# Two-layer graph block on one core: the scores' cross parts go through the attention's trip in DRAM

## The reference, cut to what matters

```
u     = h @ h.T / sqrt(384)
a     = softmax(u);  delta = a * adj
attn  = delta / (sum(delta) + 1e-10)
hl, hs, hr = h @ Wl.T + bl, h @ Ws.T + bs, h @ Wr.T + br
ctx   = (attn * upper) @ hl + diag(attn) * hs + (attn * lower) @ hr
h     = relu(layernorm(ctx, 1e-12) * g + beta)      # twice
out   = layernorm(x + h, 1e-5)
```

## Time and profile before

| | |
|---|---|
| median of 3 runs | 1637.04 us (1635.62 to 1637.73) |
| profiled execution, its own time | 1637.5 us |
| its span, first to last instruction | 1635.7 us |
| TensorE, VectorE, GpSimd, ScalarE busy | 98%, 91%, 73%, 58% of the span |
| granted TensorE clock, mean | 0.996 |
| DMA, mean busy share of 16 engines | 43% |
| one steady iteration, read from the timeline | 12.44 us |

### The profile page before, as it was taken

One profiled execution on the slowest core, in us unless ns is written; L12 is line 12 of the kernel. 1 busy time (PEld: TensorE's weight loads), 2 busy tenths in 40 slices (PEclk: granted clock), 3 DMA queues, 4 the chain that ended last, 5 costly groups with the idle time before them and its releaser, 6 DMA issues.

```text
span 1635.7 us, 35455 instructions
## 1 busy us (share of the span) xinstructions
PE 1609.5 (98%) x9505; PEld 1601.3 (98%) x9505; DVE 1491.4 (91%) x4628; ACT 951.4 (58%) x2451; POOL 1202.1 (73%) x1541
## 2 busy tenths in 40 slices
PE   8999999999999999999999999999999999999995
PEld 7999999999999999999999999999999999999995
DVE  7799999999999999999999999999999999999987
ACT  5565665556566556556656655665665556566553
POOL 5677777777777777777777777777777777777763
PEclk9999999999999999999999999999999999999998
DMA  4344444444444444444444444444444444444431
GB/s 158 94 116 107 111 111 112 106 113 114 107 114 109 111 107 113 114 107 114 110 110 107 112 115 107 114 111 110 108 111 115 107 114 111 110 109 110 114 83 44
DMA packets 463515, 178.61 MB, mean 109 GB/s; under 512 B 348545, under 2 KB 462593, under 8 KB 463490
## 3 DMA queue, kind: packets, MB, share of 16 engines
q1 hardware_dynamic: 463490, 178.32, 43.1%
HBM read 112.34 MB, written 65.86 MB: 109 GB/s over the span
## 4 chain that ended last, share of the span: by engine, by line
PE 91%; DVE 2%; DMA 1%; POOL 1%; SPq 1%; ACT 1%; issue 1%; DVEq 0%; POOLq 0%; ACTq 0%
PE p_proj L427 70%; PE p_gather L514 15%; PE p_score L421 5%; PE p_score L443 1%; DMA rows_mem<-rows_blocks 1%; DMA attnT_whole<-attn_mem 1%; SPq L366 1%; SPq L351 1%; POOL rstd L1164 0%; POOL proj_split L283 0%; POOL attnT L1154 0%; POOL attnT_split L1160 0%; DVE stats L626 0%; ACT normed L961 0%; DVE stats L672 0%
## 5 line engine op out<-in xcount | busy, mean ns | idle before, releaser
L427 PE MATMUL p_proj<-w,hT_layer 128*128 128x384 f32 x6912 | 1371.6, 339 | 0.2 <-DVE proj L697 0.2
L427 PEld LDWEIGHTS p_proj<-w,hT_layer 128*128 128x128 f32 x6912 | 1165.9, 189 | 0.5 <-DVE proj L697 0.5
L283 POOL TENSOR_TENSOR proj_split<-proj,proj_split 128x768 fp32r<-128x768 f32 x253 | 467.6, 1848 | 276.9 <-ACT proj_split L957 276.9
L957 ACT ACTIVATE proj_split<-proj 128x768 fp32r<-128x768 f32 x256 | 214.9, 839 | 394.9 <-DVE proj L697 393.8
L514 PE MATMUL p_gather<-proj_split,attnT_split 128*128 128x384 f32 x1536 | 309.2, 335 | 3.0 <-POOL attnT_split L1160 2.4
L514 PEld LDWEIGHTS p_gather<-proj_split,attnT_split 128*128 128x128 f32 x1536 | 270.0, 188 | 4.9 <-POOL attnT_split L1160 4.1
L1164 POOL TENSOR_TENSOR rstd<-veps,neg_half 128x1 f32<-128x1 f32 x384 | 211.2, 550 | 75.3 <-DVE veps L635 61.8
L697 DVE TENSOR_TENSOR proj<-p_proj,bias_all 128x768 f32<-128x768 f32 x256 | 245.1, 957 | 12.0 <-PE p_proj L427 4.4
L421 PE MATMUL p_score<-hT_layer 128*128 128x256 f32 x768 | 216.8, 283 | 2.0 <-DVE rows L729 2.0
L1154 POOL TENSOR_TENSOR attnT<-attnT_whole,sides 128x256 f32<-128x256 f32 x249 | 184.5, 741 | 41.0 <-DMA attnT_whole<-attn_mem 39.0
L1160 POOL TENSOR_TENSOR attnT_split<-attnT,attnT_split 128x256 fp32r<-128x256 f32 x256 | 190.3, 743 | 5.8 <-ACT attnT_split L948 5.8
(11 more groups left out here) (67 smaller groups left out, 1568.2 us busy)
## 6 DMA issues: line engine op xcount, KB each, us to landing
xt_raw<-xT SPq DMA_DIRECT2D x128, 192.0 KB, 2.5
xn<-x SPq DMA_DIRECT2D x128, 192.0 KB, 2.4
out<-o SPq DMA_DIRECT2D x128, 192.0 KB, 2.0
rows_mem<-rows_blocks SPq DMA_DIRECT2D x124, 192.0 KB, 1.9
rowsT<-rows_mem SPq DMA_DIRECT2D x496, 48.0 KB, 2.4
adj_layer<-adj SPq DMA_DIRECT2D x256, 64.0 KB, 1.9
attn_mem<-attn_blocks SPq DMA_DIRECT2D x124, 128.0 KB, 1.7
attnT_whole<-attn_mem SPq DMA_DIRECT2D x496, 32.0 KB, 2.2
```

The lines of the kernel that those rows point to most:

```text
L283: op.tensor_tensor(proj_split[u][:, LO], proj[u][:, UP:LOW + 1, :], proj_split[u][:, HI].bitcast(F32), ALU.subtract).then_inc(s_proj_lo[k], 1)
L427: return nc.tensor.matmul(p_proj[:, which, 0:D], hT_of(k, b)[:, slot, st, c, :], w[:, k, which, mv, c, :], start=(n == 0), stop=(n == 8))
L957: nc.scalar.activation(proj_split[u][:, HI], proj[u][:, UP:LOW + 1, :], ACT.Copy).then_inc(s_proj_hi[k], 1)
```

## The change

What it does, part by part:
- The two layers' score products stand in one PSUM bank (`parts`), and in steady state all six are issued within layer 1's self projection (`pair_slice`): layer 1 of graph i + 2 (before: i + 1, one iteration later) and layer 2 of graph i - 2. Layer 1's inputs get four slots in place of two, and are prepared an iteration earlier.
- ScalarE copies both cross parts at once (`copy_cross`, 256 columns); VectorE transposes them in blocks (`turn_cross`); they go with the attention's blocks through DRAM (256 KB stored, four loads of 64 KB). In the next iteration GpSimd adds the transposed cross parts to the plain ones (`add_cross`), and `scaled_scores` of both layers read that sum. The cross matmul is left in `fill` and `close` only.
- The orders on VectorE, ScalarE and GpSimd are changed: scores of both layers and the output's mean stand ahead of the sides' bias, both masks and diagonals behind `block_rows`; on ScalarE the exponentials stand ahead of `normalise_rows`.
- The output's mean comes from the accumulator of the sum x + h, and its variance from a pass of squares on ScalarE, in place of VectorE's statistics.
- The first layer's bias is loaded by DMA to all partitions, in place of a TensorE product with ones; the lists of `close` are reordered; a score product waits for the previous `scaled_scores` instead of the previous `diagonal`.

```diff
+        crossed = sb("crossed", [P, 2, N])
+        cross_sum = sb("cross_sum", [P, 2, N])
+        blocks = sb("blocks", [P, 2, 4, N])
+        whole = sb("whole", [P, 4, N])
...
+        parts = [p_score[0][:, 0:2, :], p_score[0][:, 2:4, :]]
+        cross_parts = p_score[0].rearrange("p (k t) n -> p k t n", t=2)[:, :, LO, :]
+        E = [p_score[1][:, 0, :], p_score[1][:, 1, :]]
...
# SyncE
+            def store_swap(i, slot):
+                first, last = swapped(i)
...
+                elif last == 4:
+                    sp.wait_ge(s_cross_blocks, i - 3)
...
+                sp.dma_start(swap_mem[slot][:, first:last], blocks[:, slot, first:last]).then_inc(
+                    s_swap_out[slot], 16)
+            def load_swap(i, slot):
+                first, last = swapped(i)
+                sp.wait_ge(s_swap_out[slot], swap_moves(i, slot))
+                pieces = swap_mem[slot].rearrange("(r a) k (s b) -> s a k r b", a=B, b=B)
...
+                        sp.dma_start(whole[rows_s, first:last, :].rearrange("a k (r b) -> a k r b", b=B),
+                                     pieces[s][:, first:last]).then_inc(s_swap_in[slot], 16)
# TensorE
+            def pair_slice(b0, slot0, b1, slot1, n):
+                if n == 2:
+                    done(pe, s_negmax[1], b1 - 1)
+                    if b0 is not None:
+                        done(pe, s_lo[0], b0)
+                        done(pe, s_negmax[0], b0 - 1)
+                if b0 is not None and 2 <= n < 2 + C:
+                    step = score_step(0, b0, slot0, n - 2)
...
+                if 2 + C <= n < 2 + 2 * C:
+                    step = score_step(1, b1, slot1, n - 2 - C)
...
-                    score0 = (0, i + 1, q) if live(i, i + 1) else None
-                    project_sides(0, i, p, 1, i - 4, range(18), score0)
-                    project_self(0, i, p, 1, i - 4)
+                    b0 = i + 2 if live(i, i + 2) else None
+                    project_sides(0, i, r, 1, i - 4, range(18))
+                    project_self(0, i, r, 1, i - 4, pair=(b0, (r + 2) % 4, i - 2, p))
                     gather(1, i - 4)
-                    project_sides(1, i - 3, q, 0, i, range(18), (1, i - 2, p))
+                    project_sides(1, i - 3, q, 0, i, range(18))
                     project_self(1, i - 3, q, 0, i)
                     gather(0, i)
# VectorE
+            def output_mean(b):
+                done(dve, s_y_nbias, b - 1)
                 done(dve, s_y, b)
-                nc.vector.bn_stats(stats6[:, 2], y_rows(b)).then_inc(s_y_stats, 1)
...
+                nc.vector.tensor_scalar(neg_mean[:, 2:3], y_sum[:], -1.0 / D, None,
+                                        ALU.mult).then_inc(s_y_mean, 1)
...
+            def turn_cross(i, slot):
+                done(dve, s_crossed, i - 4)
+                if live(i, i + 2):
+                    nc.vector.transpose(blocks[:, slot, 2:4].rearrange("p k n -> p (k n)"),
+                                        crossed[:].rearrange("p k n -> p (k n)")).then_inc(s_cross_blocks, 1)
...
                 normalise_layer1(i - 1, q)
                 low_rows(i - 2, p)
+                if not isinstance(i, int) or i > 4:
+                    done(dve, s_cross_sum, i - 5)
+                    output_mean(i - 5)
+                    if live(i, i + 1):
+                        scaled_scores(0, i + 1, q, cross_sum[:, 0])
+                    scaled_scores(1, i - 3, q, cross_sum[:, 1])
+                add_bias(0, i, True)
+                block_rows(i - 1)
                 mask(i, 1, i - 3, q)
                 if live(i, i + 1):
-                    done(dve, s_score[0], i + 1)
+                    mask(i, 0, i + 1, q)
                 diagonal(1, i - 3, q)
                 if live(i, i + 1):
-                    scaled_scores(0, i + 1, q)
-                add_bias(0, i, True)
-                block_rows(i - 1)
-                if live(i, i + 1):
-                    mask(i, 0, i + 1, q)
                     diagonal(0, i + 1, q)
+                turn_cross(i, p)
                 add_bias(0, i, False)
                 row_moments(1, i - 4, p)
...
                 output_rows(i - 4, p)
-                done(dve, s_score[1], i - 2)
                 add_bias(1, i - 3, True)
-                scaled_scores(1, i - 2, p)
-                output_moments(i - 4)
                 add_bias(1, i - 3, False)
# ScalarE
                 relu_rows(i, i - 2, p)
-                if live(i, i + 1):
-                    cross_scores(0, i + 1)
                 high_rows(i - 2, p)
-                high_sides(1, i - 4)
-                normalise_rows(i, i - 1)
                 if live(i, i + 1):
                     exponentials(0, i + 1, q)
+                exponentials(1, i - 3, q)
+                normalise_rows(i, i - 1)
+                high_sides(1, i - 4)
+                high_projections(0, i)
+                copy_cross(i)
                 high_sides(0, i)
-                high_projections(0, i)
...
                 if live(i, i - 5):
+                    output_squares(i - 5, q)
                     finish(i, q)
-                cross_scores(1, i - 2)
                 high_projections(1, i - 3)
-                exponentials(1, i - 2, p)
# GpSimd
+            def add_cross(first, last):
+                nc.gpsimd.tensor_tensor(cross_sum[:, first:last], crossed[:, first:last],
+                                        whole[:, 2 + first:2 + last], ALU.add).then_inc(s_cross_sum, 1)
...
                 low_projections(nc.gpsimd, pool, 1, i - 4)
                 attn_arrived(i - 1, q)
+                if not isinstance(i, int) or i > 4:
+                    add_cross(0, 2)
+                deviation_layer1(i - 1)
                 cut_sides(1, i - 4)
-                deviation_layer1(i - 1)
                 low_sides(1, i - 4)
                 cut_sides(0, i)
-                if live(i, i - 5):
-                    deviation_output(i - 5)
                 low_sides(0, i)
                 low_projections(nc.gpsimd, pool, 0, i)
                 deviation_layer2(i - 4)
+                if live(i, i - 5):
+                    deviation_output(i - 5)
```

More of the change, by code:

```diff
@@ L261, in attnT_count, with cross_count, swapped @@
             return b + 1 if k == 0 else b - G + 8
+        def cross_count(b):
+            return b + 1 if b < 6 else b - G + 6
         def rowsT_count(b):
             return b + 1 if b < 2 else b - G + 5
[L266 to L270, removed]
+        def swapped(i):
+            return (1, 2) if isinstance(i, int) and i == G - 1 else (0, 4)
         def done_apart(eng, s, b):
@@ L343, in load_attn @@
[L343 to L349, removed]
-                for s in range(4):
-                    sp.dma_start(AT_whole[s * B:(s + 1) * B, first:last, :].rearrange("a k (r b) -> a k r b", b=B),
-                                 blocks[s][:, first:last]).then_inc(s_attn_in[slot], 16)
+            def store_swap(i, slot):
+                first, last = swapped(i)
+                if isinstance(i, int) and i == 3:
+                    sp.wait_ge(s_blank, 1)
+                    sp.wait_ge(s_attn_blocks[0], 1)
+                elif last == 4:
+                    sp.wait_ge(s_cross_blocks, i - 3)
+                else:
+                    sp.wait_ge(s_attn_blocks[1], i - 2)
+                sp.dma_start(swap_mem[slot][:, first:last], blocks[:, slot, first:last]).then_inc(
+                    s_swap_out[slot], 16)
@@ new lines, in load_swap @@
+            def load_swap(i, slot):
+                first, last = swapped(i)
+                sp.wait_ge(s_swap_out[slot], swap_moves(i, slot))
+                pieces = swap_mem[slot].rearrange("(r a) k (s b) -> s a k r b", a=B, b=B)
+                for s in range(4):
+                    rows_s = slice(s * B, (s + 1) * B)
+                    if last - first == 1:
+                        sp.dma_start(whole[rows_s, first, :].rearrange("a (r b) -> a r b", b=B),
+                                     pieces[s][:, first]).then_inc(s_swap_in[slot], 16)
+                    else:
+                        sp.dma_start(whole[rows_s, first:last, :].rearrange("a k (r b) -> a k r b", b=B),
+                                     pieces[s][:, first:last]).then_inc(s_swap_in[slot], 16)
@@ L391, in iteration @@
                     store_rows(i - 1, q)
-                store_attn(i, p)
+                if not isinstance(i, int) or 3 <= i < G:
+                    store_swap(i, p)
                 if live(i, i - 3):
@@ L420, in score_step @@
                 h = hT_of(k, b)
-                return nc.tensor.matmul(p_score[k][:, HI:LO + 1, :], h[:, slot, HI, n, :],
+                return nc.tensor.matmul(parts[k], h[:, slot, HI, n, :],
                                         h[:, slot, HI:LO + 1, n, :], start=(n == 0), stop=(n == C - 1))
@@ L461, in project_sides, with project_self @@
                     last.then_inc(s_proj[k], 1)
```

(6 more changed lines are left out.)

339 lines of the change are left out of this document (185 added, 154 removed).

## The result

The changed kernel takes 1766.78 us (median of 4 runs, 1764.69 to 1768.43), the kernel before on the same chip 1636.33 (4 runs, 1635.05 to 1637.73): a ratio of 1.0795, 95% interval 1.0779 to 1.081, 130 us slower. The forecast was 1777 us, range 1690 to 1835.

The account below looks back on a forecast made before the run. A ring of waits through DRAM, 13.61 us, was to set the period in place of TensorE's list: 1637.5 + 122 x (13.61 - 12.44) = 143, less 3 for the ends, gives 1777 us, range 1690 to 1835.

Parts of the forecast that it names:

- Step 1: VectorE's transpose of the crossed parts until SyncE sees it: 0.47 us.
- Step 2: SyncE issues the store, 0.51 us, and x, 0.53 us, before the loads; the rows' store has already landed.
- Steps 3 and 4: SyncE's issue of four rows' loads, 2.62 us, then three of the four swap loads, 1.96 us.
- The rival with doubled issue: Swap loads' issue doubles with twice the pieces: ring 15.4 us, 1996 us in all; a longer ring had chance 0.08.
- Step 5: Landing of the last swap load, now 64 KB, until GpSimd starts: 2.75 us, bounds 2.35 and 3.4.
- the ring: Waits from VectorE's transpose through DRAM, GpSimd's sum and VectorE's scores to the next transpose: 13.61 us, setting the period.
- second ring: From VectorE's layer-2 bias through ScalarE, GpSimd's low projections and add_cross, back to that bias: 13.14 us.
- Step 6: GpSimd's add_cross, 0.74 us, and hand-over to VectorE, 0.04 us: 0.78 us.
- Step 7: VectorE's mean and first scores, then ScalarE's exponentials and normalisation, to block_rows: 1.93 us, lower end 1.36.
- Step 8: VectorE's block_rows, masks, transpose and diagonals up to the next turn_cross: 2.06 us.
- The faster rival: The ring closes inside TensorE's list; 123 x 0.24 us gained plus 3 from the ends, 1604 us; chance 0.10.
- the short ring: Landing does not grow, block_rows does not wait: 12.6 to 13.1 us, second ring rules, 1654 to 1715 us; chance 0.14.

Follow-up runs that it names:

- e1: Changed kernel with VectorE's transpose of the crossed parts ahead of both diagonals instead of behind them; 1761.77 us.
- e8: e4 with layer 2's sides cut ahead of normalise_rows on ScalarE and the masks ahead of block_rows on VectorE; 1620.37 us.
- e4: e3 with add_cross ahead of low_projections(1) on GpSimd; 1640.34 us.
- e5: e2 with both masks ahead of block_rows on VectorE; 1725.53 us.
- e2: Changed kernel with the rows' four loads issued by ScalarE, behind output_squares, instead of SyncE; 1707.92 us.
- e10: Changed kernel with the four swap loads issued by ScalarE, ahead of finish, instead of SyncE; 1711.97 us.
- e3: Changed kernel with add_cross adding the plain cross parts twice, not waiting for the swap, transposed part left out, all DMAs kept; 1684.74 us.
- e9: e10 with masks ahead of block_rows, layer 2's bias early, and layer 2's sides cut first on ScalarE and GpSimd; full computation; 1632.6 us.
- e7: e5 plus layer 2's bias before the sum with x, rows' loads ahead of output_squares, layer 2's sides cut earlier on ScalarE and GpSimd; 1800.69 us.

## Why the prediction was right

By its own steps, for the turn shown above:
- Step 1: 804.25 to 804.72, 0.47, as said.
- Step 2: store 0.55 (said 0.51), x to the first load 0.39 (said 0.53). The step takes the rows' store as landed, which holds in this turn and not in the some 40 above, where its landing released the loads. The sum came out all the same because that way is nearly as long (13.51 us, e1), which was luck.
- Steps 3 and 4: 2.65 for the rows' loads and 810.32 - 808.31 = 2.01 for three of the swap's (said 2.62 and 1.96). Twice the pieces left the issue as it was, 0.65 us for each load. The rival with doubled issue falls here, by 200 us.
- Step 5: 813.04 - 810.32 = 2.72, said 2.75. The page's median landing is 2.6 us for 64 KB behind 2.2 and 2.4: the slope held. The Trainium skill (DMA: Bandwidth & Descriptors, Anatomy of one DMA) gives 2.0 us plus bytes over 436 GB/s for a DMA that GpSimd issues, so an estimate of 2.15 us for 64 KB. These transfers were SyncE's, and their 2.6 us is 0.45 above it. The forecast's reading of it was also off: 2.15 in place of 2.75 makes the ring 13.01 us, 0.6 shorter and not 0.4, and that is under its second ring of 13.14.
- The trip in sum 8.79, said 8.84.
- Step 6: GpSimd 0.74, hand-over 0.28 in this turn where 0.04 was said (814.06 - 813.78); the chain has two of VectorE's own semaphore instructions (DVEq L249) in it. The next turn has 0.04 (827.65 - 827.61); 0.28 comes back four turns on (867.95 to 868.23), as often as the loop, unrolled four times, comes round. That is 0.06 us per turn that no step of the forecast has.
- Step 7: 814.06 to 815.98 = 1.92, said 1.93, and block_rows is released by ScalarE's `normed`, as the waits show.
- Step 8: 817.98 - 815.98 = 2.00, said 2.06.

This turn is longer than the forecast's 13.61, by the hand-over; the mean is 13.56, as the hand-over is short in three turns of four and the trip 8.66 in the short ones (303.31 to 311.97). The size: 122 x (13.61 - 13.56) = 6 us too much for the ring, 122 x (12.47 - 12.44) = 4 too much as one window of TensorE stood for the mean of before, ends -2.3 for -3. That is the 10 us between 1777 and 1767. In the forecast's bounds the upper end of the ring with step 5 high is 13.61 + 0.65 = 14.26, not 14.5; nothing hangs on it.

Three things were wrong though they cost the forecast nothing, as the ring hid them:
- The price of the cross matmul. I divided by a gather's 0.173 us and had 0.12 left. In the earlier trace rows themselves the instruction behind it starts 0.07 us later (807.64, 807.71), and the 12 projections take 0.177 each. The faster rival was worth 122 x 0.1 + 3 = 15 us, and e8 measured 16. TensorE's list alone kept the time above 1604.
- The number of rings. Two were named, 0.47 us apart. The runs found the way over the rows' store beside the first (13.51, e1), a third ring (12.44, e4), and where SyncE's loads moved to ScalarE, one more through the rows' trip (13.2, e5). "1.4 us that TensorE now has free" was only true as long as the first ring ruled.
- TensorE's busy share, a sign that was to be near 90%: it is 94%. Its list of 12.35 us in a period of 13.56 is 91%; most likely durations that overlap fill part of the waits.

Of the rivals, the short ring was right in its mechanism (with the swap freed the second ring rules, 1708 and 1712 in its span of 1654 to 1715), and wrong as a forecast of this kernel, since landing grew and block_rows waited.

That the trip is the cause is shown by e2, e10 and e3: each takes 55 to 82 us away by shortening or cutting it. That nearly all of the rest is a ring with no DMA in it is shown by e4, which took 44 of e3's last 48 us. What keeps e9's turns 0.07 us over e8's stays open.

## What to carry to other kernels

A transfer that nobody waits for is free only while its user stands an iteration behind; before a change lets an earlier instruction use the result, add up the way from that instruction round to the store of the next iteration, with every issue on the queue between, and compare the sum with the period. Then look for the next ring and the one behind it: here they stood at 13.6, 13.5, 12.9 and 12.5 us over a list of 12.4, and no single move gave back more than the step to the next. Price an instruction that is removed by the start of its follower in the timeline, not by a difference against another kind.

## What the runs showed of the hardware

- Time from issue to landing grew by about 0.2 us for each 16 KB: 2.2, 2.4 to 2.5 and 2.6 us for 32, 48 and 64 KB, in loads from DRAM cut in 128-byte pieces. It is not the bytes alone: the adjacency's 64 KB, in rows of 512 bytes, land in 1.9 us on the same page.
- The queue's time for such a load did not grow: 0.65 us with 256 pieces before and with 512 after, on SyncE and on ScalarE (2.56 to 2.69 for four). In e2, where both issued at the same time (803.13 and 803.95), SyncE's four took 2.76.
- A load issued from ScalarE takes its engine's time as work does: 2.59 us for four, and while its semaphore is open everything behind it stands (e7, 3.28 us in the iteration shown).
- GpSimd's sum of 256 columns took 0.61 us when both operands were one tile, 0.74 with two.
